# Turning the probabilities of a two-layer cross-attention in 32x32 squares on VectorE and sorting them by transfers, in place of TensorE's transposes

## The reference, cut to what matters

```
kh = concat([kh, bias_k], axis=1)        # 361 context rows and one bias row: T = 362
vh = concat([vh, bias_v], axis=1)
logits = einsum('bqhk,bthk->bhqt', qh, kh) / scale
weights = softmax(logits, axis=-1)
ctx = einsum('bhqt,bthk->bqhk', weights, vh).reshape(b, q_len, H * K)
return ctx @ wo + bo
```

## Time and profile before

| | us |
|---|---|
| median of 3 runs | 1784.81 (1784.6 to 1786.17) |
| the profiled execution's own time | 1782.94 |
| its span | 1781.1 |
| TensorE busy with matmuls | 1761.6 |
| DVE busy | 1155.0 |
| POOL busy | 843.9 |
| ACT busy | 745.3 |

### The profile page before, as it was taken

The page is one execution under the profiler, slowest core; times in us unless marked ns, Lnnn a source line. Parts: engine busy times, 40 slices in busy tenths (PEclk is TensorE's granted clock), DMA queues, the critical chain, the costliest instruction groups (busy, mean ns, idle before and its releaser), DMA issues.

```text
span 1781.1 us, 30253 instructions
## 1 busy us (share of the span) xinstructions
PE 1761.6 (99%) x11146; PEld 1715.6 (96%) x11146; DVE 1155.0 (65%) x2705; ACT 745.3 (42%) x1624; POOL 843.9 (47%) x701
## 2 busy tenths in 40 slices
PE   8999999999999999999999999999999999999999
PEld 5899999999999999999999999999999999999999
DVE  3667676666876665657766566668766665676665
ACT  3634333333553333335443333345533333344554
POOL 2774342353584352534863423535834434315554
PEclk9999999999999999999999999999999999999999
DMA  9933231122551211223522211134412122104342
GB/s 261 246 119 86 68 94 40 35 81 81 137 143 35 56 54 52 79 62 99 142 78 52 80 40 56 54 107 123 135 36 62 44 58 80 58 22 142 112 137 78
DMA packets 116165, 156.90 MB, mean 88 GB/s; under 512 B 48344, under 2 KB 63960, under 8 KB 116020
## 3 DMA queue, kind: packets, MB, share of 16 engines
q1 hardware_dynamic: 113300, 150.68, 30.1%
q10 hardware_dynamic: 2720, 4.30, 0.8%
HBM read 149.81 MB, written 5.14 MB: 87 GB/s over the span
## 4 chain that ended last, share of the span: by engine, by line
PE 91%; DVE 4%; DMA 1%; POOL 1%; ACT 1%; issue 1%; SPq 0%; ACTq 0%; DVEq 0%; POOLq 0%
PE psum L695 28%; PE psum L697 28%; PE psum L696 28%; PE psum L1019 4%; PE psum L729 2%; DMA key_stage<-head_w_dram 1%; DVE prob L1826 1%; DVE centred L1729 0%; DVE a_lo L1525 0%; ACT prob L1372 0%; DVE stats L1817 0%; PE psum L708 0%; PE psum L866 0%; PE psum L704 0%; POOL x_held L651 0%
## 5 line engine op out<-in xcount | busy, mean ns | idle before, releaser
L555 POOL TENSOR_TENSOR wbuf_hi<-stage,zero_col 128x512 fp32r<-128x512 f32 x256 | 271.8, 1062 | 694.2 <-PE psum L697 497.0
L610 POOL TENSOR_TENSOR wbuf_lo<-stage,wbuf_hi 128x512 fp32r<-128x512 f32 x256 | 334.9, 1308 | 20.1
L695 PE MATMUL psum<-pT_hi,ctx_rows_hi 121*128 121x250 f32 (+3 forms) x1152 | 332.6, 289 | 0.0
L697 PE MATMUL psum<-pT_hi,ctx_rows_lo 121*128 121x250 f32 (+3 forms) x1152 | 331.3, 288 | 0.0
L696 PE MATMUL psum<-pT_lo,ctx_rows_hi 121*128 121x250 f32 (+3 forms) x1152 | 330.8, 287 | 0.0
L695 PE MATMUL psum<-ctxT_hi,a_hi 128*125 128x362 f32 (+1 forms) x832 | 280.8, 337 | 0.4
L697 PE MATMUL psum<-ctxT_hi,a_lo 128*125 128x362 f32 (+1 forms) x832 | 272.7, 328 | 0.0
L696 PE MATMUL psum<-ctxT_lo,a_hi 128*125 128x362 f32 (+1 forms) x832 | 272.5, 328 | 0.0
L1525 DVE TENSOR_TENSOR a_lo<-psum,a_hi 128x500 fp32r<-128x500 f32 (+2 forms) x288 | 144.2, 523 | 174.1 <-ACT a_hi L1147 174.0
L695 PE MATMUL psum<-a_hi,wbuf_hi 128*128 128x400 f32 x720 | 255.2, 354 | 1.6 <-DVE xT L1744 1.6
L697 PE MATMUL psum<-a_hi,wbuf_lo 128*128 128x400 f32 x720 | 247.6, 344 | 0.0
(11 more groups left out here) (197 smaller groups left out, 3450.0 us busy)
## 6 DMA issues: line engine op xcount, KB each, us to landing
stage<-head_w_dram SPq DMA_DIRECT2D x256, 256.0 KB, 2.8
mlp_stage<-mlp_w_dram SPq DMA_DIRECT2D x32, 512.0 KB, 3.6
ctx_rows_in<-ctx_dram SPq DMA_DIRECT2D x20, 726.0 KB
ctxT_in<-ctxT_dram SPq DMA_DIRECT2D x20, 724.0 KB, 6.9
p_b<-p_scratch SPq DMA_DIRECT2D x64, 200.0 KB, 3.6
key_stage<-head_w_dram SPq DMA_DIRECT2D x22, 256.0 KB, 8.5
l0w<-l_w_dram ACTq DMA_DIRECT2D x16, 256.0 KB, 9.1
x_held<-x_scratch SPq DMA_DIRECT2D x4, 800.0 KB, 5.7
```

What stands on the lines that cost most here:

```text
L555: return nc.gpsimd.tensor_tensor(out, in_, zero_col[0:in_.shape[0], :].broadcast_to(tuple(in_.shape)), ALU.add)
L610: nc.gpsimd.tensor_tensor(lo, held, hi.bitcast(F32), ALU.subtract).then_inc(stage_free, 1)
L695: pe.matmul(out, a_h, x_hi, start=start, stop=False)
L697: return pe.matmul(out, a_l, x_hi, start=False, stop=stop)
```

## The change

1. The chunks of context rows are no longer 121, 121 and 120, but three of 128 (`TC` = 3), 384 columns in all (`W`). The score bank's columns 362 to 383 are once set to -1e30, so that their probabilities come out as zero. The context rows lie in DRAM in another order, so that partition p = 4 i + g of chunk t holds column 96 g + 32 t + i. The products of `attend` keep their number of columns.
2. Blocks for which `in_squares` is true (x = 0 always; x = 1 in the units of two blocks, save in the steps b = 0 of `LATE`) skip `turn_probs`. These are 24 + 18 = 42 of 52 blocks in a phase, 168 of 208. DVE transposes their 128x384 probabilities in place in squares of 32x32, right behind `normalise`. ACT then issues four transfers (`sort_squares`), each from 32 partitions of `prob` to all 128 partitions of a buffer (`sorted0` for x = 0; for x = 1 spare columns of `pT`), 48 KB in 128 runs of 384 bytes. `probs_hi` and `probs_lo` read that buffer in SBUF and not the PSUM bank.
3. The next user of a `prob` buffer waits for the transfers out of it (`sorted_ld`) and no longer for the transposes. `sort_squares` stands in ACT's order behind the pieces "a" for x = 0, and between the two parts of `attended_hi` for x = 1.
4. The other 40 blocks are still turned by TensorE; their `exps` write in an order that makes the same columns meet.
5. There are 3 buffers for the spread-out first rows in place of 4 (`P0_BUFS`), and 2 for the rows on their way to DRAM in place of 3 (`ROW_BUFS`). SP loads the last head's rows in a phase later in its queue.
6. In layer 0 the chunks are of 128 too; DVE sets the masked columns with two small memsets.

```diff
+def in_squares(k, b, x):
+    return x == 0 or (x == 1 and k < len(UNITS) - 1 and not (k in LATE and b == 0))
...
-P0_BUFS = 4
-ROW_BUFS = 3
+P0_BUFS = 3
+ROW_BUFS = 2
...
                 def turn_probs(k, b, x):
+                    if in_squares(k, b, x):
+                        return
...
-                    for t, (t0, t_rows) in enumerate(CHUNKS):
-                        mm = pe.transpose(bank[PT_BANK][0:t_rows, t * PT_STEP:t * PT_STEP + rows],
-                                          prob[0:rows, i % 2, t0:t0 + t_rows], ident[0:rows, 0:rows])
+                    for t in range(TC):
+                        mm = pe.transpose(bank[PT_BANK][:, t * PT_STEP:t * PT_STEP + rows],
+                                          chunk(prob[0:rows, i % 2, :], t), ident[0:rows, 0:rows])
...
+                def sort_squares(k, b, x):
+                    at = k, b, x
+                    if not in_squares(*at):
+                        return
+                    n = sorted_blocks(ph, at)
+                    act.wait_ge(squares_turned, ph * Q_LAYER + Q_AT[at] + 1)
+                    if n > 0:
+                        used_in, user = divmod(n - 1, len(BY_HELD[x]))
+                        act.wait_ge(pt_lo, used_in * S_LAYER + T_AT[BY_HELD[x][user]] + 1)
+                        act.wait_ge(p0_kept, used_in * S_LAYER + T_AT[BY_HELD[x][user]] + 1)
+                    if x == 1:
+                        wait(act, u_mm, ph * U_LAYER)
+                    for a in range(GROUPS):
+                        squares = prob[a * SQUARE:(a + 1) * SQUARE, S_AT[at] % 2, :].rearrange("i (g f) -> i g f", g=GROUPS)
+                        act.dma_start(held[x][:, a, :], squares).then_inc(sorted_ld[x], 16)
...
                         run_pieces((k, b, "a"))
+                        sort_squares(k, b, 0)
...
                         exps(k, b, 1)
                         if before is not None:
-                            attended_hi(*before)
+                            attended_hi(*before, 0, 1)
+                        sort_squares(k, b, 1)
+                        if before is not None:
+                            attended_hi(*before, 1, DC)
                         probs_hi(k, b, 0)
...
                     nc.vector.tensor_scalar(prob[0:rows, i % 2, :], prob[0:rows, i % 2, :], st[:, 3:4], None, ALU.mult)\
                         .then_inc(s_norm, 1)
+                    if in_squares(k, b, x):
+                        dve.wait_ge(s_norm, ph * S_LAYER + i + 1)
+                        nc.vector.transpose(prob[:, i % 2, :], prob[:, i % 2, :]).then_inc(squares_turned, 1)
```

More of the change, by code:

```diff
@@ L113 @@
 S_LAYER = len(S_AT)
+def in_squares(k, b, x):
+    return x == 0 or (x == 1 and k < len(UNITS) - 1 and not (k in LATE and b == 0))
+HELD = 2
+BY_PE = [at for at in TURNED if not in_squares(*at)]
+PE_AT = {at: i for i, at in enumerate(BY_PE)}
+PE_LAYER = len(BY_PE)
+IN_SQUARES = [at for at in TURNED if in_squares(*at)]
+Q_AT = {at: i for i, at in enumerate(IN_SQUARES)}
+Q_LAYER = len(IN_SQUARES)
+BY_HELD = [[at for at in IN_SQUARES if at[2] == j] for j in range(HELD)]
 PARTS = [2 if len(unit) == 2 else DC for unit in UNITS]
@@ L303, in build @@
         p0_ld = [sem(f"p0_ld{j}") for j in range(P0_BUFS)]
+        masked_s, prob_set, squares_turned = sems("masked_s prob_set squares_turned")
+        sorted_ld = [sem(f"sorted_ld{j}") for j in range(HELD)]
         y_mm, y_hi, y_done = sems("y_mm y_hi y_done")
@@ L516, in _ @@
                 load_weights(ph, W_AT["v", H - 1])
-                for h in range(H - 4, H):
+                for h in range(H - 4, H - 1):
                     load_first_probs(ph, h)
@@ L1033, in attend @@
                         out = held[:, m % per * wide:(m % per + 1) * wide]
-                        for t, (_, rows) in enumerate(CHUNKS):
-                            mm = mm3(out, chunk(r_hi[0:rows, 3 * b + t, :], m), chunk(r_lo[0:rows, 3 * b + t, :], m),
-                                     pT_hi[0:rows, t, 0:wide], pT_lo[0:rows, t, 0:wide], start=(t == 0), stop=(t == 2))
+                        for t in range(TC):
+                            mm = mm3(out, chunk(r_hi[:, TC * b + t, :], m), chunk(r_lo[:, TC * b + t, :], m),
+                                     pT_hi[:, t, 0:wide], pT_lo[:, t, 0:wide], start=(t == 0), stop=(t == TC - 1))
                         if m % per == per - 1:
@@ L1369, in exps @@
                     else:
-                        wait(act, pt_mm, ph * S_LAYER)
+                        act.wait_ge(pt_mm, used_in * PE_LAYER + PE_AT[user] + 1)
                     st = stats[0:rows, i % 2, :]
-                    nc.scalar.activation(prob[0:rows, i % 2, :], bank[S_BANK + i % 2][0:rows, 0:T], ACT.Exp,
+                    out = (in_order if in_squares(k, b, x) else sorted_columns)(prob[0:rows, i % 2, :])
+                    nc.scalar.activation(out, in_order(bank[S_BANK + i % 2][0:rows, 0:W]), ACT.Exp,
```

143 lines of the change are left out of this document (96 added, 47 removed).

## The result

The changed kernel takes 2017.91 us (median of 4 runs, 2013.94 to 2023.74), against 1784.71 for the kernel before beside it: a ratio of 1.1311 (95% interval 1.1293 to 1.1329). It is 233 us slower. The forecast was 1754 us, and no rival reached further than 1819.

The account below looks back on a forecast made before the run. TensorE, busy 1761.6 of 1781.1 us, was taken as the bound: 58 us of turns removed, 26 us back as waits, -32 from 1782.94 gives 1751, median 1753, rounded to 1754; range 1726 to 1792, likeliest case 1740 to 1772.

Parts of the forecast that it names:

- A turn: TensorE's queue: each turn of a block costs 0.345 us, so 168 turns removed save 58 us.
- the loop through ScalarE and VectorE: Step without pieces: the chain through ACT and DVE takes 10.2 us, while TensorE needs only 8.2 us.
- The transfer's landing: Sorted block, four parts: lands 3.3 us from the first issue's start; for x = 1 inside the 10.2 us.
- one of the signs of being wrong: Sign in the high part's copy: the prediction is wrong if `probs_hi` waits for a transfer more than for its turn.
- I take 0.40 and a gap of 0.04: 1.75 us for four. Bounds: 0.22 and 0.50 each.: ACT's queue: four transfer issues for each of 168 blocks cost 1.75 us; bounds 0.22 and 0.50 us each.
- Steps with two or more pieces regain it: Steps with two or more pieces make up the lag, 0.9 us a step, of steps with a k piece.
- Unit 5: ... none: Unit 5: no wait, since it has a third block's scores and 5.7 us of attend.
- 26 us: Waits before attend: 5.2 us a phase, 21 in four, plus 5 in the first, back from 58 us saved.
- The rival with an 11.8 us loop: VectorE's transpose at 1.2 us, issues at 0.45: waits of 85 and 8 us, 1819 us; chance 0.13, slower issues included.
- The k step: Step with a k piece: loop of 11.25 us against TensorE's 10.37, 0.9 us of lag a step.
- the same work from another memory ... nothing: `probs_hi` and `probs_lo`: reading SBUF, with 384 columns for 375, costs nothing extra.
- in the steps that matter most: `probs_lo` contention with GpSimd's splits: set aside because POOL is idle there, 0.00 us.

Follow-up runs that it names:

- no_sort: Changed kernel with nothing issued or transferred for the sort; VectorE still turns the squares, the high part is copied from them: 1788.0 us, 1.0018.
- one_waited: Changed kernel, but only the first of four issues carries data and is waited for; three more copy ident into an unused tile: 2013.11 us, 1.1276.
- one_issue: Changed kernel with one of each block's four transfers made, the other three and their issues left out: 1821.08 us, 1.0204.
- filled: Changed kernel with useless transposes of ident on TensorE, 20 before unit 0's attention, 16 before unit 5's turn of x = 1: 2014.28 us.

## Why the prediction was wrong

**The terms that were right.** A turn costs TensorE 0.345 us: without sorting, a step of two turns fell from 8.89 to 8.20 us. VectorE's transpose takes 0.578 us (0.60 taken). The form of the loop through ScalarE and VectorE holds in a step without pieces: with 0.63 us for each of eight issues in place of 0.44, the 10.2 us become 11.7, and 11.80 were measured. The transfer's landing is hidden in that step, as was said, though it comes some 4.0 us after the first issue (1.9 + 2.1) and not 3.3. In the steps b = 0 and 1 of `LATE` and in (5, 0) it is not hidden; that `probs_hi` waits for a transfer was one of the signs of being wrong that the prediction named.

**The first step that failed, a size:** "I take 0.40 and a gap of 0.04: 1.75 us for four. Bounds: 0.22 and 0.50 each." Four take 2.51 us. My bounds came from issues between DRAM and a tile. No row had a copy from tile to tile, and that took 0.61 us even for a single row. It was also the term that the text itself called decisive.

**The second, larger: "Steps with two or more pieces regain it", "Unit 5: ... none", "26 us".** This was an account of TensorE's and VectorE's time in each step, in which pieces cover the loop. The rival with an 11.8 us loop had about the measured loop, and by that account gave 1819, so a loop of the right length alone moves the forecast by 65 of the 264 us that it was off. Of the 233 us lost, 164 fall into the rows of the table behind its first two, where the account had next to no waits and counted the removed turns as a gain. (The third step and the granted clock, below, are part of these 164.) In (1, 1) and (3, 1), with two v pieces each, 31.6 us were lost, in unit 5 47.9, in (1, 3) and (3, 3) 35.7; only (1, 2), (3, 2), (2, 2), (4, 2) and (4, 3) regain anything. The k step failed too: 11.25 us were forecast, about 12.0 with the measured issues, and (0, 1) takes 14.9 to 16.4 (12.2 to 13.8 in `no_sort`). A piece doesn't cover ScalarE's issues, because its own high part, the attended block and the next exps are made by ScalarE, in order, behind them. ScalarE's 160 copies of attended blocks show it: it counts as idle before them for 231.2 us, and 195.1 of these are put down to the issues:

```profile
L1196 ACT ACTIVATE a_hi<-psum 128x500 fp32r<-128x500 f32 x160 | 92.3, 585 | 231.2 <-issue 195.1 <-PE psum L743 36.1
```

672 issues at 0.625 us hold the queue for 420 us, beside 751 of work that is counted as busy. `one_waited` shows that this time is most of the cost of the last three issues, and the length of the chain a small part of it.

**The third: "the same work from another memory ... nothing".** The two groups in the kernel before:

```profile
L1525 DVE TENSOR_TENSOR pT_lo<-psum,pT_hi 121x375 fp32r<-121x375 f32 x192 | 104.3, 543 | 10.0 <-ACT pT_hi L1147 2.5
...
L1839 DVE COPY p_row<-psum 1x125 f32<-1x125 f32 x192 | 51.1, 266 | 0.0
```

`probs_lo` went from 543 ns to 746 (x = 0) and 596 (x = 1), the copy of the first row from 266 to 512 and 436: 96 x 0.45 + 72 x 0.22 = 59 us more on VectorE. The prediction saw the contention for `probs_lo`, and set it aside because GpSimd was idle "in the steps that matter most". Once other steps wait too, they matter as well. Without GpSimd's splits `probs_lo` still takes 585 ns for x = 0, so some 40 of its 200 ns more have another cause, which no run parts (384 columns for 375, SBUF for PSUM).

**The order of costs**, each a difference of medians: without sorting and without squares 1749.8, 36 us under before (the removed turns are 58 us; no run took the splits away as well, so what keeps the rest isn't shown). VectorE's squares add 38, the first issue and its transfer 33, the other three issues 197. The shares depend on this order. From the other end, taking the squares away first gives back 114. The 197 have in them 54 us that TensorE is busy longer with the same instructions (1736.9 us in `one_issue`), so a part of them comes by way of the clock, as follows.

**What was not foreseen at all:** of the 232 us between the spans of `no_sort` and the changed kernel, 69 are the same 10642 instructions of TensorE, busy for 1790.8 and not 1722.0 us. The mean granted clock is 0.963 for 0.994; in the two steps after 627.57 it was 0.86 and 1.00, where before shows 1.00. In the first of the two TensorE had waited 3.06 us for `pT_lo`, until 628.74, and then worked without a pause. The matmul behind that wait, three windows of 1 us, and starts of attend in the changed kernel:

```profile
628.74 0.38 PE L741 MATMUL psum<-pT,ctx_rows_hi 128*128 128x250 f32 x1 [3.06 <-DVE pT L1607]
...
629.00:630.00 1.00, 1.00 (x7) 1.00 (x7) 0.97 (x3) 0.00 (x0) 0.00 (x0) 0.58 0.00 1
631.00:632.00 1.00, 1.00 (x7) 1.00 (x7) 0.00 (x0) 0.00 (x0) 0.00 (x0) 0.50 0.31 63
634.00:635.00 1.00, 1.00 (x10) 1.00 (x9) 1.00 (x2) 0.00 (x0) 0.00 (x0) 1.00 0.00 0
...
630.06 0.41 PE L742 MATMUL psum<-pT,ctx_rows_hi 128*128 128x250 f32 x1
630.27 0.41 PE L743 MATMUL psum<-pT,ctx_rows_lo 128*128 128x250 f32 x1
...
633.31 0.28 PE L742 MATMUL psum<-pT,ctx_rows_hi 128*128 128x250 f32 x1
633.43 0.28 PE L743 MATMUL psum<-pT,ctx_rows_lo 128*128 128x250 f32 x1
```

From about 629.2 to 632.5 the granted clock is at its lower level (0.50, 1.2 of 2.4 GHz), and attend's matmuls start 0.21 us apart in place of 0.12. `filled`, where the clock rose with a part of the waits filled, ties the clock to TensorE's waits. An estimate: means of 0.963 and 0.994 over levels of 0.5 and 1 are 149 and 21 us at the lower level; the 128 us more, of which 0.45 is lost by the starts above, make up to 58 of the 69 us. What the rest is stays open.

## What to carry to other kernels

Count an issue of a transfer as work of the engine that makes it, and add it to that engine's busy time: the profile doesn't. Price it by a row with the same two memories, and if there is none, give it a bound far above. When an in-order queue gets new work, list everything that stands behind it, in every kind of step, and ask who waits for that. Matmuls that keep TensorE busy hide nothing if their own operands have to pass through the same queue, behind the new work.

## What the runs showed of the hardware

- An issue from ScalarE of a tile-to-tile transfer takes 0.61 to 0.63 us in its queue (median), for one row of 384 bytes as for 32 rows in 128 runs; from SyncE 0.60. As a block's only issue, in `one_issue`, it takes 0.551. A row to DRAM takes 0.22.
- Each quarter of a sorted block, 48 KB in 128 runs of 384 bytes, lands 2.1 us (median) after its issue begins; a single row in 1.7.
- A transpose of squares of 128x384 fp32 takes 0.578 us on VectorE, with no spread (578 to 581 ns).
- ScalarE's exps of 384 take 0.92 to 0.95 us when they write every fourth element, and 0.56 to 0.58 when they write in order.
- A copy of 128 elements in one partition on VectorE takes 0.21 us (median), with up to 1.32 us in the changed kernel, and 1.07 without GpSimd's splits; the mean fell from 512 to 294 ns with them gone.
- Behind a wait of TensorE of 3.06 us its granted clock fell to 0.50 (from about 629.2 to 632.5 us in the changed kernel), and matmuls of 250 columns started 0.21 us apart in place of 0.12.
